# Graph attention on one core: scores in four 32-row tiles of the TensorE array, from native fp32 operands

## The chip, the cores and the metric

One core of a Trainium2 chip runs the whole program. The metric is the device time of one execution in microseconds (us), as a median of runs. The engines are PE (TensorE matmuls; PEld is its weight load), ACT (ScalarE), DVE (VectorE), POOL (GpSimd) and SP (SyncE, which here only issues DMAs). PSUM has eight banks; a bank holds 128 partitions of 512 fp32 values.

## The reference

There are 32 graphs of 256 nodes with 384 features; 12 heads of 32. All arrays are fp32.

```python
q = _split_heads(input_graph @ Wq + bq)
k = _split_heads(input_graph @ Wk + bk)
v = _split_heads(input_graph @ Wv + bv)
scores = jnp.einsum('bhqd,bhkd->bhqk', q, k) / jnp.sqrt(HD)
scores = scores + beta * adj_e
scores = jnp.where(adj_e > 0, scores, -9000000000000000.0)
probs = jax.nn.softmax(scores, axis=-1)
out = jnp.einsum('bhqk,bhkd->bhqd', probs, v)
# then: x = _layernorm(x + out)
```

## The kernel before

A **batch** is one graph. The program walks 32 batches; nearly all of them run in a loop of two. Within a batch every engine goes through 12 **steps**, one per head h. Each engine works strictly in the order in which its code is written; semaphores tie the engines together. Nothing is scheduled by a planner.

In step h, PE (`batch`, from line 437) issues the **scores** of a head three ahead (h + 3, `AHEAD`), the four 128x128 transposes of the probabilities of head h (`turn`, L396), and one **job** for the next batch. Every fourth step it adds a group of **values** (L412: probabilities times V for four heads, in four 32-column tiles of the array, native fp32), and two steps later in the cycle the transposes of a finished group (`turn_group`, L420).

The eleven jobs of a batch are, in this order: Q0, Q1, Q2, K0, K1, K2, X0, V0, X1, V1, X2. Q, K and V jobs are projections of nine matmuls each (L367), because each operand is split into a high and a low fp32r part and three products are added. X jobs transpose a third of x of the batch after next (L335). Job k is issued in step k - 1, so Q1 comes in step 0, V1 in step 8, X2 in step 9; step 10 has none and step 11 has Q0 of the following batch.

A job is written to one of two PSUM banks (`j_bank`) in turn. ACT takes it out as the high part (`high`: L486 for Q and K, L491 for V, L493 for X). For Q, K and X jobs DVE then takes out the low part (`low`: L567, L570). `project` waits for `high` and `low` of the job before the previous one (k - 2), since that is what last used the bank.

The scores are one matmul per 128 rows: the contraction of a head is only 32 long, so three products (high x high, high x low, low x high) are stacked in 96 rows of the array. The stacked operands are built by `stack_parts` on SP: once DVE has made the last low part of K2, it issues 12 DMAs (L292), SBUF to SBUF, from `qk_parts` into `stack`, three for each j = h mod 4. `scores` of the first four heads of a batch waits for `stacked[j]`. There are three score banks; head h waits until the row maxima of head h - 3 are taken.

DVE takes the row maxima (`maxima`, L557: two for each head, bias added, two heads ahead of PE's step), ACT the exponentials (`exps`, L472, one head ahead). In a step ACT does `exps` first, then a copy of transposed probabilities (`copy_turned`, L499, every third head; DVE does the others, L577), then a copy of values (`copy_group`, L506), and last `high` of the job that PE issued in the step before. POOL makes the bias and the layer norm.

Of the kernel before, what the change touches and what calls it, by code (L numbers as in the profile page):

```python
# [17 lines left out]
F32 = mybir.dt.float32  # L18
# [5 lines left out]
P = 128  # L24
PAIRED = ((0, 0), (0, 1), (1, 0))
PARTS = len(PAIRED)
# [8 lines left out]
def graph_attention_program(nc, x, adj, wq, bq, wk, bk, wv, bv, beta, out):  # L35
# [8 lines left out]
    NS = 3  # L44
    AHEAD = NS
# [8 lines left out]
    LOWS = 2 * G + C  # L54
# [9 lines left out]
    with ctx:  # L64
# [23 lines left out]
        qk_parts = sb("qk_parts", [P, 2, 4, G, N], F32R)  # L88
        stack = sb("stack", [P, 2, 2, J, G, N], F32R)
# [38 lines left out]
        first_bank = [*j_bank, t_bank[0]]  # L128
# [5 lines left out]
        stacked = [sem(f"stacked{j}") for j in range(J)]  # L134
# [60 lines left out]
        def has_low(k):  # L195
            return JOB[k][0] != "V"
# [56 lines left out]
        def _(sp):  # L253
# [44 lines left out]

            stack_parts(0, 0)

            def batch(i, par):
# [11 lines left out]
                if not is_last(i, par):  # L313
                    stack_parts(i + par, 1 - par)
# [14 lines left out]
        def _(pe):  # L329
# [40 lines left out]
            def scores(i, par, h):  # L370

                g, j = h // J, h % J
                if g == 0:

                    wait(pe, stacked[j], count(i, par, PARTS * DMA, PARTS * DMA))

                wait(pe, max_ready, count(i, par, EXPS, T * (h - NS + 1)))
                b = s_bank[h % NS]
                R = PARTS * HD
                for t in range(T):  # L380
                    mm = pe.matmul(b[:, t * N:(t + 1) * N], stack[0:R, par, 0, j, g, t * P:(t + 1) * P],  # L381
                                   stack[0:R, par, 1, j, g, :], start=True, stop=True)
                mm.then_inc(scores_ready, 1)
# [49 lines left out]
            for h in range(AHEAD):  # L433
                scores(0, 0, h)
# [28 lines left out]
        def _(act):  # L463
# [12 lines left out]
            def high(i, par, k):  # L476

                wait(act, job_ready, job_count(i, par, k))
                b = j_bank[(C + par * JOBS + k) % 2]
                if k < KV:  # L480
                    q, g = k // G, k % G
                    if k == 0:
                        for j in range(J):

                            wait(act, stacked[j], count(i, par, PARTS * DMA, -PARTS * DMA))
# [368 lines left out]
```

## Time and profile before

| what | us |
|---|---|
| median of 3 runs (lowest, highest) | 877.06 (875.73, 879.56) |
| span of the profiled execution | 871.1 |
| median less that span | 6.0 |
| PE busy (share) | 748.6 (86%) |
| DVE busy (share) | 643.6 (74%) |
| ACT busy (share) | 632.8 (73%) |
| POOL busy (share) | 420.7 (48%) |

The profile gives the span from the first to the last instruction; the time of that execution outside its span is not recorded, and the median of the runs lies 6.0 us above it. Busy time of PE is the union of its matmuls with modelled ends, so that a busy PE may still be waiting inside a matmul's drain. In a timeline row the first number is the start, the second the time from the first start to the last end of the instructions in it. The distance from one row's start to the next row's start on PE is what the first row costs there.

### The profile page before, as it was taken

The numbers are of one execution on the slowest core, as the hardware profiler recorded it, in microseconds if no ns is written. First come the engines' busy times: TensorE is split into PE (matmuls) and PEld (weight loads), VectorE is DVE, ScalarE is ACT, GpSimd is POOL, SyncE is SP. The second block draws the span as 40 slices with busy tenths as digits, with TensorE's granted clock in tenths as the row PEclk, the third lists the DMA queues.
The fourth block names the chain that finished last, engine by engine and source line by source line (L and its number), as shares of the span: only waits on it lengthen the run. The fifth ranks groups of instructions, "written<-read, shape, count | busy, mean of one in ns | idle before, by whom it ended". The sixth has DMA issues, their size and how long they took to land.

```text
span 871.1 us, 27397 instructions
## 1 busy us (share of the span) xinstructions
PE 748.6 (86%) x6528; PEld 657.1 (75%) x6528; DVE 643.6 (74%) x2487; ACT 632.8 (73%) x2116; POOL 420.7 (48%) x660
## 2 busy tenths in 40 slices
PE   5799998888988888989888989888998888999882
PEld 4678887777887777887777887777787777787761
DVE  3477777777777776877777787777877777787775
ACT  3477877777876777877777877777777777777772
POOL 1312555454555454556454556454456454456453
PEclk9899999999999999999999999999999999999997
DMA  4666444566544566544566545566544566544461
GB/s 151 140 140 140 104 119 117 137 158 155 107 118 114 137 157 156 107 117 116 133 158 157 109 119 116 129 157 158 116 118 114 124 158 157 115 118 113 96 147 36
DMA packets 59226, 111.87 MB, mean 128 GB/s; under 512 B 8704, under 2 KB 34560, under 8 KB 59136
## 3 DMA queue, kind: packets, MB, share of 16 engines
q1 hardware_dynamic: 59136, 111.05, 55.1%
q14 instruction: 80, 0.66, 0.2%
q8 instruction: 10, 0.16, 0.1%
HBM read 22.94 MB, written 12.58 MB: 41 GB/s over the span
## 4 chain that ended last, share of the span: by engine, by line
PE 35%; SPq 33%; DMA 18%; ACT 5%; issue 5%; DVE 3%; ACTq 0%; DVEq 0%
SPq L292 32%; PE j_bank L367 18%; DMA stack<-qk_parts 17%; PE t_bank L396 7%; PE s_bank L381 5%; PE o_bank L412 4%; ACT probs L472 2%; ACT qk_parts L486 2%; DVE qk_parts L567 2%; ACT probs_t L499 1%; PE o_bank L420 1%; DMA beta_col<-in_L_gnn_beta_dram 1%; ACTq L178 0%; PE j_bank L335 0%; DVE w_low L684 0%
## 5 line engine op out<-in xcount | busy, mean ns | idle before, releaser
L472 ACT ACTIVATE probs<-neg_scores,neg_max 128x256 f32<-128x256 f32 x768 | 381.9, 501 | 41.2 <-DVE neg_max L557 37.9
L557 DVE CUSTOM_DVE_ANT_0 neg_scores<-s_bank,bias_sb 128x256 f32<-128x256 f32 x768 | 290.2, 415 | 97.5 <-issue 51.6
L381 PE MATMUL s_bank<-stack 96*128 96x256 f32 x768 | 170.9, 304 | 95.5 <-DMA stack<-qk_parts 95.5
L396 PE MATMUL t_bank<-ident,probs 128*128 128x128 f32 x1536 | 231.4, 272 | 1.8 <-ACT probs L472 1.3
L381 PEld LDWEIGHTS s_bank<-stack 96*128 96x128 f32 x768 | 120.8, 190 | 125.5 <-issue 74.2
L396 PEld LDWEIGHTS t_bank<-ident,probs 128*128 128x128 f32 x1536 | 177.6, 141 | 3.3 <-ACT probs L472 1.8
L486 ACT ACTIVATE qk_parts<-j_bank,qk_bias 128x256 fp32r<-128x256 f32 x192 | 90.7, 473 | 120.6 <-PE j_bank L367 95.6
L577 DVE COPY probs_t<-t_bank 128x512 f32<-128x512 f32 x256 | 175.6, 686 | 1.1 <-PE t_bank L396 1.1
L567 DVE SCALAR_TENSOR_TENSOR qk_parts<-j_bank,qk_bias,qk_parts 128x256 fp32r<-128x256 f32 x192 | 92.4, 481 | 76.4 <-ACT qk_parts L486 76.4
L472 ACT ACTIVATION_READ_ACCUMULATOR probs<-neg_scores,neg_max 128x1 f32 x768 | 146.5, 191 | 0.0
L367 PE MATMUL j_bank<-xt_high,w_high 128*128 128x256 f32 x576 | 116.6, 311 | 6.0 <-ACT w_high L517 5.5
L810 POOL TENSOR_SCALAR o_sb<-y_sb,rstd,shift 128x384 f32<-128x384 f32 x62 | 107.8, 1744 | 11.5 <-POOL shift L804 11.5
L778 POOL TENSOR_TENSOR y_sb<-att,x_res 128x768 f32<-128x768 f32 x31 | 57.1, 1841 | 101.8 <-DVE att L593 101.8
L412 PE MATMUL o_bank<-probs_t,v_sb 128*32 128x256 f32 x1536 | 102.8, 385 | 1.0 <-DVE att L593 0.9
L367 PE MATMUL j_bank<-xt_low,w_high 128*128 128x256 f32 x576 | 99.7, 282 | 0.0
L367 PE MATMUL j_bank<-xt_high,w_low 128*128 128x256 f32 x576 | 99.5, 281 | 0.0
L367 PEld LDWEIGHTS j_bank<-xt_high,w_high 128*128 128x128 f32 x576 | 81.5, 192 | 19.2 <-DVE qk_parts L567 9.1
L367 PEld LDWEIGHTS j_bank<-xt_low,w_high 128*128 128x128 f32 x576 | 82.3, 191 | 0.0
L367 PEld LDWEIGHTS j_bank<-xt_high,w_low 128*128 128x128 f32 x576 | 81.9, 190 | 0.0
L499 ACT ACTIVATE probs_t<-t_bank 128x512 f32<-128x512 f32 x128 | 74.4, 581 | 0.9 <-PE t_bank L396 0.7
L756 POOL TENSOR_SCALAR adj_beta<-adj_sb,beta_col 128x512 f32<-128x512 f32 x32 | 64.1, 2003 | 12.5 <-DMA adj_sb<-in_adj_dram 12.5
L792 POOL TENSOR_SCALAR var_eps<-mean_var 128x2 f32<-128x2 f32 x31 | 6.0, 193 | 129.0 <-DVE mean_var L618 129.0
(59 smaller groups left out, 927.4 us busy)
## 6 DMA issues: line engine op xcount, KB each, us to landing
stack<-qk_parts SPq DMA_DIRECT2D x384, 192.0 KB, 4.0
x_sb<-in_x_dram SPq DMA_DIRECT2D x32, 384.0 KB, 4.9
out_dram<-o_sb SPq DMA_DIRECT2D x31, 384.0 KB, 4.5
adj_sb<-in_adj_dram SPq DMA_DIRECT2D x32, 256.0 KB, 4.8
w_raw<-in_L_gnn_Wq_dram SPq DMA_DIRECT2D x1, 576.0 KB, 4.2
w_raw<-in_L_gnn_Wk_dram SPq DMA_DIRECT2D x1, 576.0 KB, 6.6
w_raw<-in_L_gnn_Wv_dram SPq DMA_DIRECT2D x1, 576.0 KB, 8.2
out_dram<-o_sb SPq DMA_DIRECT2D x2, 192.0 KB, 2.0
```

The costliest lines, as they stand in the source:

```text
L292: sp.dma_start(stack[HD * n:HD * (n + 1), par, :, j, :, :].bitcast(F32), src.bitcast(F32)).then_inc(stacked[j], DMA)
L367: mm = pe.matmul(b[:, 0:n], w, a, start=(m == 0), stop=(m == len(pairs) - 1))
L381: mm = pe.matmul(b[:, t * N:(t + 1) * N], stack[0:R, par, 0, j, g, t * P:(t + 1) * P], stack[0:R, par, 1, j, g, :], start=True, stop=True)
L396: mm = pe.transpose(b[:, k * N + t * P:k * N + (t + 1) * P], probs[:, (T * h + t) % (T * NH), k * P:(k + 1) * P], ident[:, :])
L412: mm = pe.matmul(o_bank[HD * j:HD * (j + 1), 0:N], v_sb[:, par, k, h * HD:(h + 1) * HD], probs_t[:, (par * H + h) % NP, k, :], start=(k == ...
L472: nc.scalar.activation(probs[:, slot, :], neg_scores[:, slot, :], ACT.Exp, bias=neg_max[:, par, t, h:h + 1], scale=-1.0, accum_out=row_sum ...
L486: ins = nc.scalar.activation(qk_parts[:, par, 2 * q, g, :], b[:, 0:N], ACT.Identity, bias=qk_bias[:, q, g:g + 1])
L499: nc.scalar.activation(probs_t[:, (par * H + h) % NP, :, :], t_bank[h % NT][:, :].rearrange("p (k q) -> p k q", k=T), ACT.Identity).then_i ...
L557: nc.vector.tensor_tensor_reduce(neg_scores[:, (T * h + t) % (T * NH), :], s_bank[h % NS][:, t * N:(t + 1) * N], bias_sb[:, par, t, :], -1 ...
L567: ins = nc.vector.scalar_tensor_tensor(qk_parts[:, par, 2 * q + 1, g, :], b[:, 0:N], qk_bias[:, q, g:g + 1], qk_parts[:, par, 2 * q, g, :] ...
L577: nc.vector.tensor_copy(probs_t[:, (par * H + h) % NP, :, :], t_bank[h % NT][:, :].rearrange("p (k q) -> p k q", k=T)).then_inc(probs_t_v, 1)
L810: nc.gpsimd.tensor_scalar(o_sb[:, par, t, :], y_sb[:, t, :], rstd[:, t:t + 1], shift[:, t:t + 1], ALU.mult, ALU.subtract).then_inc(normed, 1)
```

## The change

- `stack`, `qk_parts` and their twelve DMAs are gone. Q and K are kept once, in fp32 (`qk`), as ACT takes them out of PSUM with the bias; DVE no longer makes low parts for Q and K.
- `scores(i, par, g)` makes four heads at once: for each half t of the rows, four matmuls with j = 0 to 3, each on 32 partitions (rows 32j to 32j + 31 of the array), native fp32, into four score banks. It stands in steps 2, 6 and 10 ahead of `turn`, and waits for the maxima of all four heads of the group before.
- Eight banks are shared out anew: four score banks, two for transposes, one for values, and **one** `j_bank`. `project` waits for `high` and `low` of the previous job (k - 1).
- On DVE, in steps 2, 6 and 10, the maxima come behind the copy and the low part, not ahead of them.
- Before the first batch, `scores` of four heads replace three single heads; the three first transposes of x use `j_bank` and both banks of transposes.

```diff
-        s_bank = [bank(f"s_bank{n}") for n in range(NS)]
+        s_bank = [bank(f"s_bank{n}") for n in range(J)]
         t_bank = [bank(f"t_bank{n}") for n in range(NT)]
         o_bank = bank("o_bank")
-        j_bank = [bank(f"j_bank{n}") for n in range(2)]
+        j_bank = bank("j_bank")
...
         def has_low(k):
-            return JOB[k][0] != "V"
+            return JOB[k][0] == "X"
...
-            def stack_parts(i, par):
-                multiplied = held(count(i, par, STEPS, -STEPS))
-                wait(sp, low_ready, low_count(i, par, KV - 1))
-                take_wait(sp, passed_s)
-                wait(sp, scores_ready, multiplied)
-                for j in range(J):
-                    for n, (q_part, k_part) in enumerate(PAIRED):
-                        src = qk_parts[HD * j:HD * (j + 1), par, q_part:2 + k_part + 1:2 + k_part - q_part, :, :]
-                        sp.dma_start(stack[HD * n:HD * (n + 1), par, :, j, :, :].bitcast(F32),
-                                     src.bitcast(F32)).then_inc(stacked[j], DMA)
...
             def project(i, par, k, weights_low=0):
-                b = j_bank[(C + par * JOBS + k) % 2]
-                free_bank(job_count(i, par, k - 2), low_count(i, par, k - 2))
-                if k == 0:
-                    wait(pe, low_ready, low_count(i, par, -1))
+                b = j_bank
+                free_bank(job_count(i, par, k - 1), low_count(i, par, k - 1))
...
-            def scores(i, par, h):
-                g, j = h // J, h % J
-                if g == 0:
-                    wait(pe, stacked[j], count(i, par, PARTS * DMA, PARTS * DMA))
-                wait(pe, max_ready, count(i, par, EXPS, T * (h - NS + 1)))
-                b = s_bank[h % NS]
-                R = PARTS * HD
-                for t in range(T):
-                    mm = pe.matmul(b[:, t * N:(t + 1) * N], stack[0:R, par, 0, j, g, t * P:(t + 1) * P],
-                                   stack[0:R, par, 1, j, g, :], start=True, stop=True)
-                mm.then_inc(scores_ready, 1)
+            def scores(i, par, g):
+                wait(pe, high_ready, job_count(i, par, G + g))
+                wait(pe, max_ready, count(i, par, EXPS, T * J * g))
+                for t in range(T):
+                    for j in range(J):
+                        rows = slice(HD * j, HD * (j + 1))
+                        mm = pe.matmul(s_bank[j][:, t * N:(t + 1) * N], qk[rows, par, 0, g, t * P:(t + 1) * P],
+                                       qk[rows, par, 1, g, :], start=True, stop=True)
+                        if t == T - 1:
+                            mm.then_inc(scores_ready, 1)
...
                 for h in range(H):
-                    if h + AHEAD < H:
-                        scores(i, par, h + AHEAD)
-                    elif not is_last(i, par):
-                        scores(i + par, 1 - par, h + AHEAD - H)
+                    if h % J == 2 and h < H - J:
+                        scores(i, par, h // J + 1)
+                    elif h % J == 2 and not is_last(i, par):
+                        scores(i + par, 1 - par, 0)
                     turn(i, par, h)
...
             def high(i, par, k):
                 wait(act, job_ready, job_count(i, par, k))
...
-                    ins = nc.scalar.activation(qk_parts[:, par, 2 * q, g, :], b[:, 0:N], ACT.Identity, bias=qk_bias[:, q, g:g + 1])
+                    ins = nc.scalar.activation(qk[:, par, q, g, :], b[:, 0:N], ACT.Identity, bias=qk_bias[:, q, g:g + 1])
...
                 for h in range(H):
-                    if h + 2 < H:
-                        maxima(i, par, h + 2)
-                    elif not is_last(i, par):
-                        maxima(i + par, other, h + 2 - H)
+                    if h % J != 2:
+                        maxima_ahead(i, par, h)
...
                     for job in jobs_at(i, par, h - 1):
                         if has_low(job[2]):
                             low(*job)
+                    if h % J == 2:
+                        maxima_ahead(i, par, h)
```

On PE, steps 1 and 2 of a batch read as follows before (names: `s_bank` scores, `t_bank` transposed probabilities, `j_bank` jobs, `o_bank` values):

```order
L381 MATMUL s_bank<-stack 128x256 x2
L396 MATMUL t_bank<-ident,probs 128x128 x4
L367 MATMUL j_bank<-xt_high,w_high 128x256 x3
L367 MATMUL j_bank<-xt_low,w_high 128x256 x3
L367 MATMUL j_bank<-xt_high,w_low 128x256 x3
L381 MATMUL s_bank<-stack 128x256 x2
L396 MATMUL t_bank<-ident,probs 128x128 x4
L412 MATMUL o_bank<-probs_t,v_sb 32x256 x8
L367 MATMUL j_bank<-xt_high,w_high 128x256 x3
```

And with the change:

```order
L366 MATMUL t_bank<-ident,probs 128x128 x4
L339 MATMUL j_bank<-xt_high,w_high 128x256 x3
L339 MATMUL j_bank<-xt_low,w_high 128x256 x3
L339 MATMUL j_bank<-xt_high,w_low 128x256 x3
L350 MATMUL s_bank<-qk 128x256 x8
L366 MATMUL t_bank<-ident,probs 128x128 x4
L382 MATMUL o_bank<-probs_t,v_sb 32x256 x8
L339 MATMUL j_bank<-xt_high,w_high 128x256 x3
```

The score pair of step 1 and the pair of step 2 are gone, and eight score matmuls stand together at the head of step 2.

On PE, from the end of job V0 (step 6) to the start of job V1 (step 8), before:

```order
L367 MATMUL j_bank<-w_low,xt_high 128x384 x3
L381 MATMUL s_bank<-stack 128x256 x2
L396 MATMUL t_bank<-ident,probs 128x128 x4
L335 MATMUL j_bank<-ident,x_sb 128x128 x2
L381 MATMUL s_bank<-stack 128x256 x2
L396 MATMUL t_bank<-ident,probs 128x128 x4
L420 MATMUL o_bank<-ident,heads_t 128x128 x2
L367 MATMUL j_bank<-w_high,xt_high 128x384 x3
```

And with the change:

```order
L339 MATMUL j_bank<-w_low,xt_high 128x384 x3
L366 MATMUL t_bank<-ident,probs 128x128 x4
L310 MATMUL j_bank<-ident,x_sb 128x128 x2
L366 MATMUL t_bank<-ident,probs 128x128 x4
L390 MATMUL o_bank<-ident,heads_t 128x128 x2
L339 MATMUL j_bank<-w_high,xt_high 128x384 x3
```

Two score pairs that stood between a job and the next one have left this stretch; what is left between two jobs is one `turn`, and between X1 and V1 a `turn` and a `turn_group`.

## Rows read from the trace of the kernel before

**Rows 1.** Page: engines (busy us, share, instructions); granted clock per slice.

```profile
PE 748.6 (86%) x6528; PEld 657.1 (75%) x6528; DVE 643.6 (74%) x2487; ACT 632.8 (73%) x2116; POOL 420.7 (48%) x660
...
PEclk9899999999999999999999999999999999999997
```

**Rows 2.** Chain of waits, one batch: start us, us, what.

```profile
397.92 0.12 issue
398.04 0.50 PE s_bank L381 x2
...
409.82 0.63 SPq L292
...
419.26 4.72 DMA stack<-qk_parts
```

**Rows 3.** Timeline of PE: start us, us, work, count, idle before; score stalls.

```profile
418.00 0.50 PE L381 MATMUL s_bank<-stack 96*128 96x256 f32 x2 [0.76 <-DMA stack<-qk_parts]
...
420.61 0.50 PE L381 MATMUL s_bank<-stack 96*128 96x256 f32 x2 [0.68 <-DMA stack<-qk_parts]
...
424.10 0.50 PE L381 MATMUL s_bank<-stack 96*128 96x256 f32 x2 [1.50 <-DMA stack<-qk_parts]
```

**Rows 4.** Sum of waits of the whole span: total us, times, longest.

```profile
PE s_bank L381 <- DMA stack<-qk_parts: 95.5, 96, 2.8
```

**Rows 5.** Timeline of PE: scores, turns, a projection and a values group.

```profile
400.11 0.40 PE L381 MATMUL s_bank<-stack 96*128 96x256 f32 x2
400.35 0.60 PE L396 MATMUL t_bank<-ident,probs 128*128 128x128 f32 x4
400.70 0.60 PE L367 MATMUL j_bank<-xt_high,w_high 128*128 128x256 f32 x3
...
402.08 0.60 PE L396 MATMUL t_bank<-ident,probs 128*128 128x128 f32 x4
402.61 1.07 PE L412 MATMUL o_bank<-probs_t,v_sb 128*32 128x256 f32 x16
403.61 0.61 PE L367 MATMUL j_bank<-xt_high,w_high 128*128 128x256 f32 x3
```

**Rows 6.** Inside that values group: PE timeline at two short windows.

```profile
402.61 0.42 PE L412 MATMUL o_bank<-probs_t,v_sb 128*32 128x256 f32 x4
...
402.85 0.61 PE L412 MATMUL o_bank<-probs_t,v_sb 128*32 128x256 f32 x8
```

**Rows 7.** Weight loads by line: count, duration ns min/median/max, span, form.

```profile
L412 PEld LDWEIGHTS o_bank<-probs_t,v_sb x1472: 106/110/110, 64.5 to 848.5; 128*32 128x32 f32 x184
...
L381 PEld LDWEIGHTS s_bank<-stack x738: 186/189/192, 59.9 to 849.8; 96*128 96x128 f32 x185
```

**Rows 8.** Timelines of PE, ACT and DVE: who frees the projection banks.

```profile
400.31 0.47 ACT L486 ACTIVATE qk_parts<-j_bank,qk_bias 128x256 fp32r<-128x256 f32 x1 [0.45 <-PE j_bank L367]
...
404.94 0.47 ACT L486 ACTIVATE qk_parts<-j_bank,qk_bias 128x256 fp32r<-128x256 f32 x1 [0.73 <-PE j_bank L367]
...
405.35 0.60 PE L367 MATMUL j_bank<-xt_high,w_high 128*128 128x256 f32 x3
...
406.69 0.47 ACT L486 ACTIVATE qk_parts<-j_bank,qk_bias 128x256 fp32r<-128x256 f32 x1 [0.29 <-PE j_bank L367]
...
407.31 0.60 PE L367 MATMUL j_bank<-xt_high,w_high 128*128 128x256 f32 x3
...
413.01 0.49 ACT L491 ACTIVATE v_sb<-j_bank 128x384 f32<-128x384 f32 x1 [1.22 <-PE j_bank L367]
...
413.49 0.38 PE L335 MATMUL j_bank<-ident,x_sb 128*128 128x128 f32 x2
...
414.53 0.77 PE L367 MATMUL j_bank<-w_high,xt_high 128*128 128x384 f32 x3
...
415.27 0.42 DVE L570 TENSOR_TENSOR xt_low<-j_bank,xt_high 128x256 fp32r<-128x256 f32 x1 [1.00 <-ACT xt_high L493]
```

**Rows 9.** Timeline of PE before the first batch: the second score stall.

```profile
30.61 0.80 PE L381 MATMUL s_bank<-stack 96*128 96x256 f32 x2 [2.82 <-DMA stack<-qk_parts]
```

More of the change, by code:

```diff
@@ L24 @@
 P = 128
-PAIRED = ((0, 0), (0, 1), (1, 0))
-PARTS = len(PAIRED)
 MASKED = -9.0e15
@@ L43, in graph_attention_program @@
     STEPS = H
-    NS = 3
-    AHEAD = NS
     NH = 3
@@ L53, in graph_attention_program @@
     V_DONE = JOB.index(("V", T - 1))
-    LOWS = 2 * G + C
+    LOWS = C
     KV = 2 * G
@@ L87, in graph_attention_program @@
         xt_low = sb("xt_low", [P, 2, C, N], F32R)
-        qk_parts = sb("qk_parts", [P, 2, 4, G, N], F32R)
-        stack = sb("stack", [P, 2, 2, J, G, N], F32R)
+        qk = sb("qk", [P, 2, 2, G, N])
         v_sb = sb("v_sb", [P, 2, T, D])
@@ L121, in bank @@
             return ctx.enter_context(nc.psum_tensor(name, [P, 512], F32))
-        s_bank = [bank(f"s_bank{n}") for n in range(NS)]
+        s_bank = [bank(f"s_bank{n}") for n in range(J)]
         t_bank = [bank(f"t_bank{n}") for n in range(NT)]
         o_bank = bank("o_bank")
-        j_bank = [bank(f"j_bank{n}") for n in range(2)]
-        first_bank = [*j_bank, t_bank[0]]
+        j_bank = bank("j_bank")
+        first_bank = [j_bank, *t_bank]
         assert len(first_bank) == C
@@ L133, in graph_attention_program @@
         adj_in = [sem(f"adj_in{n}") for n in range(2)]
-        stacked = [sem(f"stacked{j}") for j in range(J)]
         out_done = [sem(f"out_done{n}") for n in range(2)]
@@ L297, in store @@
                 sp.dma_start(out_v[2 * i + par], o_sb[:, par, :, :]).then_inc(out_done[par], DMA)
-            stack_parts(0, 0)
             def batch(i, par):
@@ L312, in batch @@
                     load_adj(i + 1, par)
-                if not is_last(i, par):
-                    stack_parts(i + par, 1 - par)
                 if not first:
@@ L432, in _ @@
                     project(0, 0, k)
-            for h in range(AHEAD):
-                scores(0, 0, h)
+            scores(0, 0, 0)
             project(0, 1, 0)
@@ L478, in high @@
                 wait(act, job_ready, job_count(i, par, k))
-                b = j_bank[(C + par * JOBS + k) % 2]
+                b = j_bank
                 if k < KV:
@@ L482, in high @@
                     if k == 0:
-                        for j in range(J):
-                            wait(act, stacked[j], count(i, par, PARTS * DMA, -PARTS * DMA))
-                    ins = nc.scalar.activation(qk_parts[:, par, 2 * q, g, :], b[:, 0:N], ACT.Identity, bias=qk_bias[:, q, g:g + 1])
+                        wait(act, scores_ready, count(i, par, STEPS, -STEPS))
+                    ins = nc.scalar.activation(qk[:, par, q, g, :], b[:, 0:N], ACT.Identity, bias=qk_bias[:, q, g:g + 1])
                 elif JOB[k][0] == "V":
@@ L557, in maxima @@
                     nc.vector.tensor_tensor_reduce(
-                        neg_scores[:, (T * h + t) % (T * NH), :], s_bank[h % NS][:, t * N:(t + 1) * N], bias_sb[:, par, t, :],
+                        neg_scores[:, (T * h + t) % (T * NH), :], s_bank[h % J][:, t * N:(t + 1) * N], bias_sb[:, par, t, :],
                         -1.0, BIG, ALU.add, ALU.min, neg_max[:, par, t, h:h + 1]).then_inc(max_ready, 1)
@@ L563, in low @@
                 wait(dve, high_ready, job_count(i, par, k))
-                b = j_bank[(C + par * JOBS + k) % 2]
-                if k < KV:
-                    q, g = k // G, k % G
-                    ins = nc.vector.scalar_tensor_tensor(qk_parts[:, par, 2 * q + 1, g, :], b[:, 0:N], qk_bias[:, q, g:g + 1],
-                                                         qk_parts[:, par, 2 * q, g, :].bitcast(F32), ALU.add, ALU.subtract)
-                else:
-                    ins = nc.vector.tensor_tensor(xt_low[:, 1 - par, JOB[k][1], :], b[:, 0:N],
-                                                  xt_high[:, 1 - par, JOB[k][1], :].bitcast(F32), ALU.subtract)
-                ins.then_inc(low_ready, 1)
+                nc.vector.tensor_tensor(xt_low[:, 1 - par, JOB[k][1], :], j_bank[:, 0:N],
+                                        xt_high[:, 1 - par, JOB[k][1], :].bitcast(F32), ALU.subtract).then_inc(low_ready, 1)
             def copy_turned(i, par, h):
@@ L697, in _, with maxima_ahead @@
                 maxima(0, 0, h)
+            def maxima_ahead(i, par, h):
+                if h + 2 < H:
+                    maxima(i, par, h + 2)
+                elif not is_last(i, par):
+                    maxima(i + par, 1 - par, h + 2 - H)
             def batch(i, par):
```

## The prediction

> **What bounds the kernel now.** I read the page first. PE is the busiest engine and its clock stands at the higher of its two levels (2.4 GHz) in nearly every slice of the span [rows 1], but no engine is full. So the next view is the chain of waits, for one batch in the middle. Its first and last links are a score matmul behind a landing DMA: from 398.04 in [rows 2] to 424.10 in [rows 3], a period of **26.06 us**. The chain inside it goes through PE, ACT and DVE to the last low part of K, then through SP, which issues its twelve DMAs one after another from 409.82 on, and the last of them takes 4.72 us to land [rows 2]. The transfers of the stacked Q and K set the period. PE's timeline shows the price on PE: it stands idle ahead of three score pairs of the batch, 0.76 + 0.68 + 1.50 = 2.94 us [rows 3]; over the span such waits sum to 95.5 us [rows 4]. The rest of a batch is PE work without a gap, some 23 us. So removing the transfers makes PE the bound, and the question is what PE does and waits for afterwards.
>
> **Part 1, the stall goes.** 2.94 us for each batch. A pair after a stall also runs longer: 0.50 us from first start to last end [rows 3] against 0.40 in an unstalled one [rows 5], three times, so 0.3 more. Part 1: -3.24 us.
>
> **Part 2, the score matmuls.** Out go 12 pairs. A pair costs PE 0.24 us (from 400.11 to 400.35 [rows 5]): -2.88. In come three groups of eight native fp32 matmuls. The trace has no row-tiled matmul, but it has the values group: also eight native fp32 matmuls of 256 columns in four tiles (column tiles), which the profile shows as 16 instructions. It holds PE for 1.00 us (402.61 to 403.61), and the `turn` ahead of it costs 0.53 instead of 0.35 (402.08 to 402.61 against 400.35 to 400.70), so 1.18 us in all [rows 5]. Four start together and the next four about 0.23 us later [rows 6]: the four tiles run side by side. One thing differs: a score tile loads 128 columns of weights, a values tile 32. Loads of 128 columns take 189 ns, of 32 columns 110 ns [rows 7]. If the four tiles load side by side, only the first load of a group is exposed, 0.08 us more: **1.26 us for a group**, 3.78 for a batch. The lower bound is the busy 1.00 alone, if a switch of tiles costs nothing; the upper one is rival B. I take 1.26 because the values group is the nearest thing in the trace. Part 2: +0.90 us.
>
> The Trainium skill ("TensorE: Matmul & The Clock Gate", Part 3) reports 3.07 times the throughput for four row tiles. As an estimate from it, eight matmuls one by one, each two instructions of 0.23 us, are 3.7 us, and a 3.07th of that is 1.2 us: the values group again. No run here shows it yet.
>
> **Part 3, one bank for the jobs.** This is a new wait. With two banks, job k waits for the bank of k - 2, and no row shows PE waiting there for long. With one it waits for ACT's `high` of job k - 1 (and for DVE's `low` after X jobs). The trace tells when that would be free. I take ACT's end, add 0.12 us until PE starts (the "issue" ahead of a released score pair [rows 2]), and compare with the time at which PE is ready for the job: its start in the trace, less the 0.24 us of the score pair that now no longer stands between two jobs.
> - Q2: ACT ends Q1 at 400.31 + 0.47 = 400.78, so free at 400.90. PE is ready at 400.70 - 0.24 = 400.46 [rows 5, 8]. Wait 0.44.
> - K1: free at 404.94 + 0.47 + 0.12 = 405.53, ready at 405.35 - 0.24 = 405.11 [rows 8]. Wait 0.42.
> - X1: free at 413.01 + 0.49 + 0.12 = 413.62, ready at 413.49 - 0.24 = 413.25 [rows 8]. Wait 0.37. X0 and X2, the same pattern, give 0.35 and 0.37.
> - K2 has a `turn_group` in between: free at 406.69 + 0.47 + 0.12 = 407.28, ready at 407.31 - 0.24 = 407.07 [rows 8]. Wait 0.21. Q1 has the same neighbours: 0.21.
> - V1 is the dear one. ACT does in order V0's `high`, the exponentials of a head, a copy, and only then X1's `high`; DVE's low part follows and ends at 415.27 + 0.42 = 415.69, free at 415.81. PE is ready at 414.53 less two score pairs, plus the 0.37 that X1 was late: 414.42 [rows 8]. Wait **1.39**.
> - K0 and V0 have scores, `turn` and a values group between them and the job before; Q0 of the next batch has two whole steps. Nothing there, unless `high` were over 2 us late.
>
> Sum: 0.44 + 0.42 + 3 waits of 0.35, 0.37 and 0.37 + 2 x 0.21 + 1.39 = **3.76 us** a batch. ACT's place in its own order does not move, so these waits don't shrink when PE gets faster; they grow.
>
> **Part 4, edits with nothing on the path.** DVE loses its low parts of Q and K; it is busy 74% [rows 1] and the maxima it makes are two heads ahead. That cover would be gone if PE stood ready before DVE; it doesn't. The maxima moved behind the copy in steps 2, 6 and 10 can only start when a score group is there; the head they serve is turned two steps later, about 3.5 us, against two maxima and two exponentials. The wait for all four banks in step 2 is for maxima that DVE did in step 1. Queued behind it on PE are `turn` and values, so it would cost at once if DVE were a step late. SP loses twelve issues, and its loads and stores only move forward. Before the first batch, PE stalled on the stack too (2.82 us at the second pair [rows 9], 5.1 in three); the single bank adds up to ten exchanges of 0.5 to 0.8 us to eleven jobs there. I set this against each other: 0, within 4 us. The last batch has no jobs: 0.
>
> **The sum.** -3.24 + 0.90 + 3.76 = +1.42 us a batch. 31 batches have it: +44. On the profiled span 871.1 that is 915.1, and with the 6.0 us that lie between that span and the median, **921 us**: 5% slower. The change trades a wait of 3.2 us for waits of 3.8 us and adds score work.
>
> **Rivals.**
> - **B, the loads of four row tiles come one after another.** 16 loads of 128 columns at the 0.12 us that half a score pair takes [rows 5] are 1.92 us, with the 0.26 around them 2.18: 0.92 more a group, 2.76 a batch, +86: 1007 us. For it: each load is four times as wide as those of the values group. Against it: there 16 loads of 0.11 us [rows 7] fit into 1.00 us [rows 5], so loads of different tiles overlap. It decides as soon as four loads outlast one round of 0.23 us. The Trainium skill (same page, "LDWEIGHTS") says that a 32x128 load takes as long as a 128x128 one, which speaks against this change; its Part 3 says that loads overlap where the row groups differ, which speaks against B. By the first rule alone the sum would be B's.
> - **C, the change doesn't do what it says: tiles run one at a time.** 16 x 0.23 + 0.26 = 3.94 a group, +2.68, 8.0 a batch: 1170 us. Rows 6 speak against it, for columns.
> - **D, faster.** The bank exchange is hidden, because PE's other work covers ACT's `high`. Then the sum is -2.34 a batch, 31 of them -73: so 871.1 - 73 + 6 = 804 us. It turns faster as soon as the waits of part 3 sum to less than 2.34 us. Against it are six separate readings in [rows 8], and most of all the order of ACT in front of V1.
> - **E, no change.** Groups at 1.00 us (-0.78 a batch) and exchanges 0.1 shorter each (-0.8) give -0.2 a batch, 872 us.
>
> **How the numbers follow.** Forecast 0.64 (880 to 960 us: groups from 1.0 to 1.6 us, waits from 3.3 to 4.5), B 0.13, C 0.05, D 0.10, E 0.08. The range takes in E, the forecast and B's lower part, where the loads queue but half hide: 872 to 1000. Left out are D, C and half of B. A measurement of this kernel can tell some 0.5% from no change, 872.7 to 881.4: faster 0.10, same 0.08, slower 0.82.
>
> **What would show it.** In the trace after: no stack DMA and no PE wait for one; a score group of 16 instructions that costs PE about 1.26 us from start to the next `turn`, with four starts together; seven waits of 0.2 to 0.45 us ahead of jobs, for ACT, and one near 1.4 ahead of V1, for DVE's low part; a period of 27.5 us. A score group of 2 us or more shows B. A period below 26 with no waits ahead of jobs shows D, and the step that failed would be part 3. If the waits are there but a group costs well under 1 us, part 2 was too dear.

## The result and the profile after

The changed kernel took **1005.05 us** (1002.93 to 1006.07, 4 runs) against 877.07 us of the kernel before on the same chip (875.73 to 879.56, 4 runs): a ratio of **1.146** (95% interval 1.1435 to 1.1488). It is slower, as forecast, but nearly three times as much as the forecast 5%, and just outside the range of 872 to 1000. The profiled execution has a span of 1004.1 us where the forecast had 915.1.

The page of the changed kernel: the engines' busy times, then TensorE's granted clock in 40 slices. It answers to [rows 1].

```profile
PE 850.0 (85%) x7296; PEld 663.2 (66%) x7296; DVE 578.1 (58%) x2295; ACT 624.2 (62%) x2116; POOL 415.4 (41%) x660
...
PEclk9999998989989899898999989899898998989998
...
PE 52%; ACT 20%; issue 19%; DVE 5%; ACTq 2%; DMA 1%; DVEq 1%; SPq 0%
```

The clock row has an 8 in 13 of its 40 slices; before it was 9 nearly throughout. The last row is the chain that ended last, by engine. ACT has 20% of it, and 19% is "issue": time in which the engine on the chain waited for nothing that the profile shows. The forecast had neither.

The view of summed waits (engine, tile and line, what was waited for: us in total, times, longest) says where. The third row is the exchange ahead of V1 that was forecast. The first two were not forecast: waits of up to 4.8 and 4.4 us.

```profile
PE j_bank L339 <- ACT qk L454: 68.9, 33, 4.8
ACT probs L441 <- issue: 56.0, 13, 4.4
...
PE j_bank L339 <- DVE xt_low L532: 34.0, 32, 1.2
```

**An ordinary batch** is close to the forecast. PE's timeline (start us, us, work, count, idle before and its releaser) around one score group: the jobs K1, K2 and X0 ahead of it and V0, X1 and V1 behind; it answers to [rows 5] and [rows 8]:

```profile
499.63 0.60 PE L366 MATMUL t_bank<-ident,probs 128*128 128x128 f32 x4
500.36 0.62 PE L339 MATMUL j_bank<-xt_high,w_high 128*128 128x256 f32 x3
...
501.53 0.60 PE L366 MATMUL t_bank<-ident,probs 128*128 128x128 f32 x4
501.96 0.38 PE L390 MATMUL o_bank<-ident,heads_t 128*128 128x128 f32 x2
502.26 0.62 PE L339 MATMUL j_bank<-xt_high,w_high 128*128 128x256 f32 x3
...
503.42 0.60 PE L366 MATMUL t_bank<-ident,probs 128*128 128x128 f32 x4
504.15 0.44 PE L310 MATMUL j_bank<-ident,x_sb 128*128 128x128 f32 x2
504.52 1.15 PE L350 MATMUL s_bank<-qk 32*128 32x256 f32 x16
505.59 0.66 PE L366 MATMUL t_bank<-ident,probs 128*128 128x128 f32 x4
506.18 1.07 PE L382 MATMUL o_bank<-probs_t,v_sb 128*32 128x256 f32 x16
507.18 0.79 PE L339 MATMUL j_bank<-w_high,xt_high 128*128 128x384 f32 x3
...
508.85 0.60 PE L366 MATMUL t_bank<-ident,probs 128*128 128x128 f32 x4
509.68 0.44 PE L310 MATMUL j_bank<-ident,x_sb 128*128 128x128 f32 x2 [0.23 <-ACT v_sb L459]
...
510.43 0.38 PE L390 MATMUL o_bank<-ident,heads_t 128*128 128x128 f32 x2
511.87 0.79 PE L339 MATMUL j_bank<-w_high,xt_high 128*128 128x384 f32 x3 [1.06 <-DVE xt_low L532]
```

The score group holds PE from 504.52 to 505.59, 1.07 us. V1 starts 1.44 us after the `turn_group` at 510.43.

**A batch with the loop's jump back** is another matter. In the kernel the loop's body is two batches, so every second batch ends with the jump. The first X job of the batches starts at 442.72 and, two batches later, at 504.15: 61.43 us for two. The one without the jump takes 27.29 us from first `turn` to first `turn`, the one with it 34.15, which is 6.86 more. The loop's body runs 14 times, so it jumps back 13 times, and the trace has 13 long batches and 13 such gaps of ACT (the second row above). Some of the expectations below count 14 jumps. ACT's timeline at one jump, then PE's:

```profile
518.19 0.37 ACT L474 ACTIVATE heads_t<-o_bank 128x256 f32<-128x256 f32 x1
522.78 0.51 ACT L441 ACTIVATE probs<-neg_scores,neg_max 128x256 f32<-128x256 f32 x1 [4.22 <-issue]
```

```profile
519.32 0.38 PE L390 MATMUL o_bank<-ident,heads_t 128*128 128x128 f32 x2
524.36 1.00 PE L339 MATMUL j_bank<-xt_high,w_high 128*128 128x256 f32 x3 [4.66 <-ACT qk L454]
525.16 0.84 PE L339 MATMUL j_bank<-xt_low,w_high 128*128 128x256 f32 x3
525.80 0.84 PE L339 MATMUL j_bank<-xt_high,w_low 128*128 128x256 f32 x3
526.45 1.05 PE L366 MATMUL t_bank<-ident,probs 128*128 128x128 f32 x4
527.21 1.01 PE L339 MATMUL j_bank<-xt_high,w_high 128*128 128x256 f32 x3
...
529.43 1.67 PE L350 MATMUL s_bank<-qk 32*128 32x256 f32 x16
531.03 0.66 PE L366 MATMUL t_bank<-ident,probs 128*128 128x128 f32 x4
```

ACT starts nothing for 4.22 us, though its operands are there. PE needs the job bank, and with one bank it waits for ACT's `high`: 4.66 us idle. Then PE runs on at the clock's lower level for some microseconds: this job's nine matmuls take 2.09 us (524.36 to 526.45), those of the same kind at 500.36 take 1.17. The 6.86 us can be counted up against the batch before, which has no jump. From the `turn_group` to this job it is 5.04 us (519.32 to 524.36) instead of 0.62 (492.04 to 492.66): 4.42 more. The work from there to the end of the score group takes 6.67 us (524.36 to 531.03) instead of 4.22 (492.66 to 496.88): 2.45 more, at the lower clock. Busy times of the engines in two stretches of 10 us (the granted clock is the last number but two):

```profile
500.00:510.00 10.00, 9.51 (x85) 7.29 (x83) 6.27 (x25) 7.13 (x25) 6.37 (x4) 1.00 0.30 99
...
520.00:530.00 10.00, 5.64 (x26) 5.25 (x30) 1.39 (x5) 4.83 (x16) 7.99 (x13) 0.69 0.11 41
```

The DMA view of 518 to 524 us, queues and their packets, names what moves in that gap: instructions, four packets of 8 KB, and nothing else. The other twelve gaps have three or four each.

```profile
q14 instruction: 4, 0.03, 2.1%
```

**The kernel before had such a gap too**, on DVE and not on ACT. Its summed waits and DVE's row at a jump (13 of the 14 waits are these, 3.9 to 4.0 us each; the last is one of 0.16 us behind the loop):

```profile
DVE neg_scores L557 <- issue: 51.6, 14, 4.0
```

```profile
450.54 0.42 DVE L557 CUSTOM_DVE_ANT_0 neg_scores<-s_bank,bias_sb 128x256 f32<-128x256 f32 x1 [4.03 <-issue]
```

There it cost next to nothing: PE sat in a stack wait until 450.27 anyway (1.60 us), and the maxima that it needed next were already there.

### The profile page after: what moved, and what is told of

Its sections match the earlier page's. It is cut to its first block, busy times and chain, and to the rows that moved or that the text cites. A ratio compares the mean times of both kernels' runs of the same rounds, so it can differ in the third digit from the quotient of the medians.

```text
span 1004.1 us, 27942 instructions
## 1 busy us (share of the span) xinstructions
PE 850.0 (85%) x7296; PEld 663.2 (66%) x7296; DVE 578.1 (58%) x2295; ACT 624.2 (62%) x2116; POOL 415.4 (41%) x660
## 4 chain that ended last, share of the span: by engine, by line
PE 52%; ACT 20%; issue 19%; DVE 5%; ACTq 2%; DMA 1%; DVEq 1%; SPq 0%
PE j_bank L339 29%; PE s_bank L350 11%; ACT probs L441 8%; PE o_bank L382 5%; ACT qk L454 5%; PE t_bank L366 5%; PE j_bank L310 3%; ACT probs_t L467 3%; ACT v_sb L459 2%; DVE neg_scores L525 2%; ACTq L172 2%; DVE xt_low L532 1%; ACT xt_high L461 1%; ACT heads_t L474 1%; DMA w_raw<-in_L_gnn_Wv_dram 1%
## 5 line engine op out<-in xcount | busy, mean ns | idle before, releaser
L366 PE MATMUL t_bank<-ident,probs 128*128 128x128 f32 x1536 | 244.3, 283 | 3.8 <-ACT probs L441 2.4
L339 PE MATMUL j_bank<-xt_high,w_high 128*128 128x256 f32 x576 | 130.8, 339 | 82.1 <-ACT qk L454 68.9
L454 ACT ACTIVATE qk<-j_bank,qk_bias 128x256 f32<-128x256 f32 x192 | 90.4, 471 | 88.1 <-PE j_bank L339 88.1
L350 PE MATMUL s_bank<-qk 32*128 32x256 f32 x1536 | 116.0, 418 | 0.1
L532 DVE TENSOR_TENSOR xt_low<-j_bank,xt_high 128x256 fp32r<-128x256 f32 x93 | 39.5, 425 | 122.7 <-ACT xt_high L461 122.7
L339 PE MATMUL j_bank<-xt_high,w_low 128*128 128x256 f32 x576 | 109.6, 303 | 0.0
L339 PEld LDWEIGHTS j_bank<-xt_high,w_low 128*128 128x128 f32 x576 | 91.9, 211 | 0.0
L350 PEld LDWEIGHTS s_bank<-qk 32*128 32x128 f32 x1536 | 74.0, 198 | 19.9 <-issue 14.0
L459 ACT ACTIVATE v_sb<-j_bank 128x384 f32<-128x384 f32 x64 | 31.3, 490 | 88.0 <-PE j_bank L339 88.0
L339 PE MATMUL j_bank<-w_high,xt_high 128*128 128x384 f32 x192 | 50.9, 373 | 34.0 <-DVE xt_low L532 34.0
```

The lines of the kernel that those rows point to most:

```text
L339: mm = pe.matmul(b[:, 0:n], w, a, start=(m == 0), stop=(m == len(pairs) - 1))
L350: mm = pe.matmul(s_bank[j][:, t * N:(t + 1) * N], qk[rows, par, 0, g, t * P:(t + 1) * P], qk[rows, par, 1, g, :], start=True, stop=True)
L366: mm = pe.transpose(b[:, k * N + t * P:k * N + (t + 1) * P], probs[:, (T * h + t) % (T * NH), k * P:(k + 1) * P], ident[:, :])
L454: ins = nc.scalar.activation(qk[:, par, q, g, :], b[:, 0:N], ACT.Identity, bias=qk_bias[:, q, g:g + 1])
L459: ins = nc.scalar.activation(v_sb[:, par, t, :], b[:, 0:D], ACT.Identity)
L532: nc.vector.tensor_tensor(xt_low[:, 1 - par, JOB[k][1], :], j_bank[:, 0:N], xt_high[:, 1 - par, JOB[k][1], :].bitcast(F32), ALU.subtract). ...
```

## The experiments

The theory after the two traces: the miss is the loop's jump. At each jump ACT is held up by the fetch of its instructions, and the single job bank passes this on to PE in full. The rivals: the row-tiled scores cost more than the group shows (rival B in part), or the single bank costs more per batch than summed.

**e1, the changed kernel, its loop written out.**

```
-            with eng.Fori(1, PAIRS - 1) as i:
+            for i in range(1, PAIRS - 1):
```

> The changed kernel with its loop of two batches written out, on all engines: same work, same order, no jump back. Theory (the 84 us beyond the forecast are paid at the 14 jumps): every batch takes the 27.3 us that the batches without a jump take now, 14 times 6.86 us go, about 909 us. Rival (something in the batches themselves, as a slower clock or a dearer score group): the time stays within 1% of 1005 us.

Measured: 909.98 us (907.04 to 911.47), ratio 1.035 (1.0312 to 1.0395). The span is 908.0, 96.1 less than with the loop. Of this 13 times 6.86 are 89; the other 7 are spread over 27 batches, which take 0.26 us less each without the loop (27.03 instead of 27.29). The clock stays at its higher level:

```profile
PEclk9999999999999999999999999999999999999998
```

In PE's timeline the same job of two batches, two batches apart, is now 54.06 us apart instead of 61.43, 27.03 a batch:

```profile
460.47 0.44 PE L310 MATMUL j_bank<-ident,x_sb 128*128 128x128 f32 x2
...
514.53 0.44 PE L310 MATMUL j_bank<-ident,x_sb 128*128 128x128 f32 x2
```

Nothing about scores or banks differs from the changed kernel. The loop is the miss, and its jumps are 89 of the 96 us. What the 0.26 us a batch are was not found out; they stay in e10, which has the loop and no gap.

**e2, the kernel before, its loop written out** (the same edit).

> The kernel before, loop written out. Theory: its jumps cost nothing, since all its batches take the same 26.1 us, with and without a jump (the 4.0 us gap of DVE lies in the shadow of the stack transfers): same within 0.5%, 873 to 881 us. Rival (a loop costs several us at each jump in any kernel): 820 us or less.

Measured: 868.47 us (867.61 to 871.26), ratio 0.990 (0.9859 to 0.9933). That is 5 us below the range that was expected, though still no change at 2%. The jumps cost at most the 5.5 us of span that went, 0.4 each, where they cost the changed kernel 6.86 each.

**e3, the changed kernel, ACT's loop alone written out**; the other engines keep theirs.

```
-            walk(act, batch)
+            walk(act, batch, unrolled=True)
```

> The changed kernel, loop written out on ACT alone; PE, DVE, POOL and SP still jump. Theory (ACT's gap is the one that is waited for, through the single job bank): nearly all of the gain of the full unrolling, 905 to 925 us. Rival (DVE's or PE's jump costs as much): most of the 6.86 us a jump stays, 970 us or more.

Measured: 913.96 us (2 runs), ratio 1.040; span 912.0. Of the 96.1 us, 92 go with ACT's loop. So it is ACT's jump; those of the other engines are worth 4 us together.

**e4 and e6, the kernel before with one job bank**, once with its loop and once written out. Scores stay as they were.

```
-        j_bank = [bank(f"j_bank{n}") for n in range(2)]
+        j_bank = [bank("j_bank")]
...
-                b = j_bank[(C + par * JOBS + k) % 2]
-                free_bank(job_count(i, par, k - 2), low_count(i, par, k - 2))
+                b = j_bank[0]
+                free_bank(job_count(i, par, k - 1), low_count(i, par, k - 1))
```

> The kernel before with one projection bank only (the eighth bank lies idle), loop kept, scores and stack as before. Theory (part 3 of the prediction): the projections Q1 to K2 lie on the chain that feeds the stack, and exchanging a single bank costs 0.2 to 0.45 us at each, V1 1.4: 1.3 to 2 us a batch, and on top jumps that are now exposed by up to 5 us: 920 to 1000 us, with long and short periods in turn. Rival (the exchange is hidden): 880 us and even periods.

> The kernel before with one projection bank, loop written out. Theory (e4 paid both the exchanges and the exposed jumps): the short periods of e4, 27.6 to 27.9 us, for every batch: 925 to 935 us, against 868 with two banks. Rival (e4's time is all exchange): stays near 1000 us.

Measured: with the loop 1000.97 us, ratio 1.139 (1.134 to 1.1448); written out 944.26, ratio 1.077 (1.0748 to 1.0793). The first is at the upper end of what was expected, the second lies 9 us above it. The single bank alone makes the kernel before as slow as the changed one. 56 us of that are the loop, and here the gap is DVE's. The summed waits of e4, then DVE and PE at one jump:

```profile
DVE neg_scores L557 <- issue: 31.5, 32, 4.3
```

```profile
638.90 0.42 DVE L557 CUSTOM_DVE_ANT_0 neg_scores<-s_bank,bias_sb 128x256 f32<-128x256 f32 x1 [4.20 <-issue]
...
640.73 1.01 PE L367 MATMUL j_bank<-xt_high,w_high 128*128 128x256 f32 x3 [2.68 <-DVE qk_parts L567]
```

Six of the 32 waits in the sum are such gaps, the rest are of 0.3 us or less. At the other seven jumps DVE stands idle as long, 3.8 to 4.6 us, and the view puts it down to the score matmul that ended last.

With two banks this gap was hidden; with one, PE needs DVE's low part of Q and K before the next job. Without jumps the single bank costs 944.26 - 868.47 = 75.8 us here, about 64 of it in the batches (27.9 against 25.8) and 11 ahead of the first batch (the first `turn` starts at 46.4 against 35.4).

**e5 and e8, the changed kernel with its jobs in another order** (X1, ahead of V1, moved away from it), written out and with the loop.

```
-    JOB = [(kind, g) for kind in "QK" for g in range(G)] + [("X", 0), ("V", 0), ("X", 1), ("V", 1), ("X", 2)]
+    JOB = [("Q", 0), ("Q", 1), ("X", 0), ("Q", 2), ("K", 0), ("K", 1), ("X", 1), ("K", 2), ("V", 0), ("V", 1), ("X", 2)]
```

> The changed kernel, loop written out, with the eleven jobs in another order: Q0 Q1 X0 Q2 K0 K1 X1 K2 V0 V1 X2, so that each X job is followed by a step that opens with a score group. Theory (part 3: V1 waits 1.4 us because X1's high part stands behind exponentials and a copy on ACT; behind a score group the wait is covered): 1.4 us a batch less than e1, about 866 us. Rival (the place of the X jobs doesn't matter, the exchange is paid wherever it is): 905 us or more.

> The job order of e5, with the loop kept. Theory (a jump costs what ACT's gap exceeds the slack of the single bank by; the order of jobs changes nothing at the jump): 14 times 5 to 7 us on e5, 935 to 965 us. Rival (the dear wait ahead of V1 used up the slack, and with it gone the jumps hide): within 15 us of e5.

Measured: written out 873.2 us (870.02 to 874.27), ratio 0.997 (0.9948 to 0.9986); with the loop 959.3, ratio 1.094 (1.0916 to 1.0969). In this order V1 follows V0, and X2 follows V1. The period of e5 is 25.72 against e1's 27.03: 1.31 us less a batch, the size of V1's wait, and the timelines show it there: V1 starts 0.31 us after its `turn_group` in e5 (471.96 to 472.27), where it takes 1.57 in e1 (520.69 to 522.26). The other waits only change places; they sum to about as much as before. The time is 7 us above the 866 that were expected. The loop costs e8 86 us over e5, against the 95 of e1's comparison: the gap is not tied to one order of the jobs.

**e7, every score group computed twice**, otherwise e1. The result is the same; PE does eight more matmuls a group.

```
-                for t in range(T):
+                for again in range(2):
+                    for t in range(T):
```

> The changed kernel, loop written out, with every score group computed twice into the same banks (the result is that of the second). It costs the eight matmuls by themselves. Theory (four row tiles side by side, four rounds of 0.22 us): +0.9 us a group, 3 groups, 31 batches: +80 to +90 us on e1, 990 to 1000 us. Rival B of the prediction (loads one after another): +1.9 us a group, 1085 us or more. If less than 60 us is added, PE is not what bounds there.

Measured: 992.57 us, ratio 1.132 (1.1299 to 1.1344); period 29.61, 2.58 more than e1, 0.86 us for eight matmuls. PE's timeline shows the doubled group:

```profile
502.15 2.01 PE L351 MATMUL s_bank<-qk 32*128 32x256 f32 x32
504.09 0.66 PE L367 MATMUL t_bank<-ident,probs 128*128 128x128 f32 x4
```

1.94 us from its start to the `turn`, against 1.07 for a single one: 0.87 for the eight. The page of e7 gives 184 ns for one of their weight loads:

```profile
L351 PEld LDWEIGHTS s_bank<-qk 32*128 32x128 f32 x3072 | 148.1, 184 | 21.4 <-issue 11.0
```

Sixteen of these one after another would take 2.9 us. So the four tiles run side by side, loads and all. Rival B (2.18 us a group) and rival C (3.94) fall.

**e10 to e14, the changed kernel with n instructions more on ACT ahead of its loop** that only add to a semaphore nobody waits for. The loop, the work and the order stay; only the place of the loop's code moves. The Trainium skill ("Runtime: NRT & Kernel Launch", "Instruction fetch mechanics") says that a taken branch whose target is not in the current window of two pages has to fetch it first, and that 16 KiB are 256 instructions.

```
+            for _ in range(32):
+                act.sem_inc(padded, 1)
             walk(act, batch)
```

> The changed kernel, with its loop, and 32 instructions more on ACT ahead of the loop that do nothing but add to a semaphore nobody waits for. Theory 1 (the 4.2 us in which ACT stands at each jump back of its loop depend on where the loop's code lies in memory, so they can move or go when it is shifted): ACT's idle time at the jump changes, and with it the time, down to about 915 us if it vanishes from ACT. Theory 2 (a jump back costs ACT this time wherever the code lies, and before it was hidden or not there because ACT came early): the gap stays at 4.0 to 4.4 us and the time at 1000 to 1010 us.

> As the run with 32, with 64 more instructions ahead of ACT's loop. Theory 1 (place of the code): another gap than in the runs with 0, 32 and 96, and a time between 915 and 1005 us that follows it. Theory 2 (any jump costs it): 4.0 to 4.4 us of gap and 1000 to 1010 us.

> As the run with 32, with 96 more instructions ahead of ACT's loop. Theory 1 (place of the code): another gap than in the runs with 0, 32 and 64, and a time between 915 and 1005 us that follows it. Theory 2 (any jump costs it): 4.0 to 4.4 us of gap and 1000 to 1010 us.

> The changed kernel with its loop and 128 more instructions ahead of ACT's loop. With 32, 64 and 96 of them the time was 920 to 926 us and ACT's gap at the jump was gone. Theory 1a (what matters is where the body lies against blocks of the size in which the trace shows instructions fetched, 8192 bytes, 128 instructions if one has 64 bytes): 128 is one whole block, the body lies as in the changed kernel, the gap of 4 us comes back and the time is 1000 to 1010 us. Theory 1b (the blocks are larger, or any shift at all helps, by a change in time): no gap, 920 to 930 us.

> The changed kernel with 16 more instructions ahead of ACT's loop. Theory 1a (a block border that the body crosses only at some offsets): either the gap is there as with none (1000 to 1010 us) or it is gone as with 32 (915 to 930 us), and nothing between. Rival (the gap shrinks as the body is moved on): about half of it, near 960 us.

| instructions added | 0 | 16 | 32 | 64 | 96 | 128 |
|---|---|---|---|---|---|---|
| time, us | 1005.05 | 917.75 | 920.09 | 924.17 | 926.04 | 1008.27 |
| ratio | 1.146 | 1.048 | 1.049 | 1.054 | 1.056 | 1.151 |
| instruction packets, q14 | 79 | 13 | 13 | 13 | 14 | 79 |

With 32, ACT's timeline at a jump has no gap, and the page counts 13 instruction packets where the changed kernel has 79:

```profile
508.99 0.37 ACT L475 ACTIVATE heads_t<-o_bank 128x256 f32<-128x256 f32 x1
509.25 0.50 ACT L442 ACTIVATE probs<-neg_scores,neg_max 128x256 f32<-128x256 f32 x1
```

```profile
q14 instruction: 13, 0.11, 0.0%
```

With 128 the gap and the packets are back:

```profile
525.69 0.37 ACT L475 ACTIVATE heads_t<-o_bank 128x256 f32<-128x256 f32 x1
530.28 0.51 ACT L442 ACTIVATE probs<-neg_scores,neg_max 128x256 f32<-128x256 f32 x1 [4.22 <-issue]
```

```profile
q14 instruction: 79, 0.65, 0.2%
```

So sixteen idle instructions make the changed kernel 87 us faster, and 128 make it as slow as with none. What decides is where the loop's code lies. A gradual effect falls: e14 is not near 960 us, and e11 and e12 have no gap of another length, as they were expected to, but none. A mere shift of ACT in time falls too, since 128 shift it most. The added instructions are themselves executed once, ahead of the loop: the trace has ACT idle for 3.93 us there with 64, 6.09 with 96 and 8.24 with 128. That goes with the slow rise from 918 to 926 us.

Theory 1a, blocks of 128 instructions, fits all six runs, but one return of the gap does not prove a period. Blocks of 256 would fit them too, if the gap stayed from 128 added instructions on to 256; no run has more than 128. The packets are 8 KB each, and that is 128 instructions at the 64 bytes that the two figures of the Trainium skill give. The mechanism of the Trainium skill fits these runs. The size of a block and how many are held were not measured.

**e15, the same shift by 32 for DVE**, in e4.

> The kernel before with a single job bank (e4: 1001.0 us with its loop, 944.3 with the loop written out, gaps of 3.4 to 4.2 us on DVE at the jumps) and 32 more instructions ahead of DVE's loop. If DVE's gap goes as ACT's did: 945 to 960 us. If DVE's body crosses a border at any offset (it is longer than ACT's): 1000 us again.

Measured: 991.97 us (2 runs), ratio 1.133; e4 had 1000.97. Where the 9 us went was not looked into. DVE's gap stays, in its timeline at a jump:

```profile
514.83 0.42 DVE L558 CUSTOM_DVE_ANT_0 neg_scores<-s_bank,bias_sb 128x256 f32<-128x256 f32 x1 [4.23 <-issue]
```

DVE has more instructions than ACT (2487 against 2116 over the span). Whether another shift would clear it, or none does, was not tried and stays open.

**e9 and e16, jobs on borrowed banks.** The order of e5; in addition the jobs of two steps in four go to score banks whose maxima are taken. Only one job in four now follows another on the same bank, and a score group and a `turn` stand between the two. e9 has its loop written out, e16 has the loop and 32 instructions ahead of ACT's.

```
+        def job_bank(k):
+            return {2: j_bank, 3: s_bank[0], 0: s_bank[1], 1: j_bank}[step_of(k) % J]
...
-                free_bank(job_count(i, par, k - 1), low_count(i, par, k - 1))
+                b = job_bank(k)
+                back = 1 if step_of(k) % J == 2 else 2
+                free_bank(job_count(i, par, k - back), low_count(i, par, k - back))
...
+                if step_of(k) % J in (3, 0):
+                    wait(pe, max_ready, count(i, par, EXPS, T * (step_of(k) + 2) - (2 if k == 0 else 1) * EXPS))
...
```

> The changed kernel with its loop written out and the jobs in the order of e5 (873.2 us, period 25.72), and in addition the jobs of the steps 3, 7 and 11 go to the first score bank and those of the steps 0, 4 and 8 to the second, once the maxima of these banks are taken, so that no job follows another on one bank within a step. Theory (the single bank's exchanges are what e5 still pays): of the 3.76 us of exchanges that the prediction summed, e5 took out those of V1 and of some of the others, period 27.03 to 25.72; the rest goes here, some 1.3 to 1.7 us a batch, so a period near 24.2 and 805 to 825 us. Rival (the exchanges are hidden behind something else by now, ACT for instance, which is busy next): the period stays at 25.5 or more, 865 to 875 us.

> The kernel of e9 (jobs in another order, and two of four jobs on score banks that are free) with its loop instead of the loop written out, and 32 instructions more ahead of ACT's loop. If the place of the code is all that the loop costs: e9's 807.6 us and the 10 us that the changed kernel still has between written out (910) and shifted by 32 (920), so 810 to 825 us. If the gap on ACT is back, in this code or on another engine: 860 us or more.

Measured: e9 807.59 us (804.95 to 808.32), ratio 0.920 (0.9168 to 0.9236), period 23.99. e16 **795.34 us** (793.75 to 796.13), ratio **0.907** (0.9058 to 0.9091), period 23.51. Both beat both kernels, and e16 is 15 us faster than the fastest that was expected. The page of e16:

```profile
PE 758.1 (95%) x7296; PEld 626.1 (79%) x7296; DVE 573.2 (72%) x2295; ACT 618.2 (78%) x2116; POOL 415.3 (52%) x660
...
PEclk9999999999999999999999999999999999999997
...
q14 instruction: 13, 0.11, 0.0%
...
PE 92%; ACT 3%; issue 2%; DVE 1%; DMA 1%; SPq 0%; DVEq 0%; ACTq 0%
```

PE is 95% busy and has 92% of the chain. So the row-tiled scores are worth having once neither the bank nor the jump stands in the way. The kernel before was not run with its jobs in this order, so how much of the gain is the order's stays open. e16, with a loop, has a period 0.48 us shorter than e9 without one, while it is the other way round for the changed kernel (27.3 in e10, 27.03 in e1). The timelines show the place: from each X job to the score group behind it e9 takes 0.60, 0.49 and 0.51 us, e16 0.40, 0.31 and 0.42, which is 0.47 less. A score group now waits for ACT to empty the borrowed banks; e9 has 32 such waits, e16 has 5. Their summed waits, e9 and then e16:

```profile
PE s_bank L370 <- ACT qk L474: 7.6, 32, 0.5
```

```profile
PE s_bank L371 <- ACT qk L475: 2.7, 5, 1.0
```

Why ACT comes earlier in e16 stays open.

## Why the prediction was wrong, step by step

**What bounds the kernel now**: right. The stack waits are gone from the trace after, and PE and its waits set the period.

**Part 1, the stall goes (-3.24 us a batch)**: no PE wait for a stack transfer is left, and the period below comes out near the sum. It was not measured apart.

**Part 2, a group at 1.26 us**: right within 0.1. Measured are 1.07 us from start to the next `turn` and 0.59 instead of 0.53 for the `turn` ahead of the values. The work ahead of a group takes longer too: an X job takes 0.37 there (504.15 to 504.52), where two transposes took 0.14 before (413.49 to 413.63, [rows 8] and the score pair behind it). That is 1.07 + 0.06 + 0.23 = 1.36 us. Behind a projection the last three matmuls take 0.44 instead of 0.36, and the sum is 1.21. Two of the three groups stand behind an X job. The forecast of 1.26 lies between; the three sum to 3.93 against its 3.78.

**Part 3, the exchanges (3.76 us a batch)**: right in place and size. V1 starts 1.44 us after the `turn_group` ahead of it, where an undisturbed job starts 0.14 after it: 1.30 against the forecast 1.39. X1 starts 0.83 us after its `turn` instead of 0.43: 0.40 against 0.37. X0, 0.73 us (503.42 to 504.15): 0.30 against 0.35. K1, 0.73 instead of 0.35 (499.63 to 500.36): 0.38 against 0.42. K2, 0.30 instead of 0.14 (501.96 to 502.26): 0.16 against 0.21. These five sum to 2.54, the forecast had 2.74 for them. All eight, read in a batch of e1, sum to 3.52 against 3.76. e5 confirms V1's: its order takes 1.31 us out of the period.

**Part 4 (0, within 4 us)**: the prologue was worse. The first `turn` starts at 36.5 us before, at 42.5 in the changed kernel and at 43.3 in e1: 6.0 and 6.8 us later, outside the bound. PE waits there behind single exchanges of 0.56 to 1.02 us (e1).

**The sum, "31 batches have it"**: this step failed. It took all batches for alike and added +1.42 to a period of 26.06: 27.48. It so put the loop's jump back at nothing, without giving a reason. The batches without a jump bear the period out, 27.29 in the changed kernel, 27.03 in e1. But 13 batches take 34.15, 6.86 more, 89 us in all; with the 0.26 us of 27 batches, 7 us, the loop costs 96.1 us, as e1 measures. The account of the span: 915.1 forecast, 31 x (27.03 - 27.48) = -14 for the batches, +6.9 for the prologue and the ends, +96.1 for the loop, 1004.1 measured.

What stood in the traces: the kernel before had a row of waits of DVE for "issue", 13 of them of 4 us each, one for every jump, and the prediction didn't read it. Whoever does would ask two things of the change. Does it take away the slack that hides this gap? It does: with one job bank PE waits for ACT within half a microsecond of every job. And does it move code? It does, and so ACT's loop, which had no such gap before, came to lie where it has one. The first could be estimated: a gap of 4 us on ACT or DVE, less the 0.4 or so of slack, is 47 us for 13 jumps. Measured were 89: PE's wait grew by 4.42 us at a jump, and 2.45 more went at the lower clock. The second could not be told from the trace of before. Without the gap on ACT the forecast would have held: e14 and e10 have 917.75 and 920.09 us against 921. That they are so close is partly luck: their batches take some 0.2 us less than the forecast 27.48, and their first `turn` starts 5 to 8 us later than before.

**The rivals.** B and C fall by e7 and by the row of the group. D, the exchange hidden, was wrong as a forecast for this kernel, but its sum of 804 us is close to what e9 has, 807.59, once most exchanges are hidden. E, no change, falls by e1, where the exchanges and the score work, with no jump at all, leave it 3.5% slower. No rival held the jump, and the upper end of the range, drawn from B, missed the measured time by 5 us, for another reason.

## What to carry to other kernels

Where a kernel has a loop, look at the batch with the jump back apart from the others, on every engine, before multiplying a period by a count: a row of waits for "issue" that come once for each jump is a cost that some slack now hides. Taking away a buffer takes away that slack first. And when a changed loop is slower by a few microseconds a jump, shift its code by a few idle instructions, or write the loop out, before judging the change itself: here 16 of them made 1.048 of 1.146. For DVE in e15 a shift by 32 did not help.

## What was not expected of the hardware

- A jump back of the loop held ACT for 4.2 us, or not at all, by the place of its code: gap at 0 and 128 added instructions, none at 16, 32, 64 and 96. Three or four instruction packets of 8 KB moved in each gap; without gaps the page counts 13 or 14 for the whole span instead of 79.
- The gap costs more than its length. Of the 6.86 us of span at a jump 4.42 are PE's longer wait and 2.45 slower work behind it, since PE came back at the clock's lower level: the granted clock is 0.69 from 520 to 530 us.
- Four row tiles of 32 rows run side by side though each loads 128 columns of weights: eight native fp32 matmuls of 256 columns in 0.87 us more (e7), less than the 1.00 us of the values group in [rows 5]. The work on either side of a group takes 0.14 to 0.29 us longer for it.
